# Products with the identity in transposing mode, and the second attention's probabilities normalised in place

## What is computed

```python
# _L0_cond2_ref: the conditioned layer, H = 16 heads of DH = 128
x1 = _ln(x) * (1.0 + scale1) + shift1
qkv = (x1 @ qkv_w + qkv_b).reshape(Bc, Tc, 3, H, DH)
q, k, v = (qkv[:, :, 0], qkv[:, :, 1], qkv[:, :, 2])
scale = DH ** (-0.5)
attn = jnp.einsum('bthd,bshd->bhts', q, k) * scale
attn = jax.nn.softmax(attn, axis=-1)
attn_out = jnp.einsum('bhts,bshd->bthd', attn, v).reshape(Bc, Tc, INNER)
...
x = x + _L0_attn_ref(_L0_cond_ref(cond_2048, cond_2048, x, L0_cond_coupling, L0_cond_bias), L0_attn_Wqkv_w, L0_attn_Wqkv_b)
x = x + _L0_ffn_ref(_L0_cond2_ref(x, cond_2048, ...), ...)
```

## Time and profile before

| | us |
|---|---|
| median of three runs (lowest, highest) | 6142.88 (6142.48, 6146.08) |
| the profiled execution | 6141.46 |
| its span, first to last instruction | 6139.8 |

### The profile page before, as it was taken

One profiled execution on the slowest core, in us unless ns is written; L12 is line 12 of the kernel. 1 busy time (PEld: TensorE's weight loads), 2 busy tenths in 40 slices (PEclk: granted clock), 3 DMA queues, 4 the chain that ended last, 5 costly groups with the idle time before them and its releaser, 6 DMA issues. The chain is left out here.

```text
span 6139.8 us, 221854 instructions
## 1 busy us (share of the span) xinstructions
PE 4707.2 (77%) x82040; PEld 4113.7 (67%) x82040; DVE 4180.4 (68%) x26093; ACT 2342.0 (38%) x10351; POOL 1733.9 (28%) x5906
## 2 busy tenths in 40 slices
PE   6777777777777777777689962999999999269888
PEld 5666666666666666666578861778777877158777
DVE  8999999999999999999756634544454444521122
ACT  3333333333333333333355522544444444222232
POOL 2333333333333333333332202222222122200000
PEclk6555555555555555555599965999999999579999
DMA  1000000000000000000200024222232232230211
GB/s 63 1 1 1 1 1 1 1 1 1 1 1 1 1 1 1 1 1 1 70 8 22 33 77 137 90 97 93 96 103 96 89 102 82 103 124 27 93 37 41
DMA packets 121590, 260.62 MB, mean 42 GB/s; under 512 B 10276, under 2 KB 10532, under 8 KB 121112
## 3 DMA queue, kind: packets, MB, share of 16 engines
q1 hardware_dynamic: 85072, 173.09, 8.2%
q0 software_dynamic: 13104, 48.26, 2.3%
q10 hardware_dynamic: 23064, 35.84, 1.8%
HBM read 194.20 MB, written 62.97 MB: 42 GB/s over the span
## 5 line engine op out<-in xcount | busy, mean ns | idle before, releaser
L211 PE MATMUL bank<-tanh_parts,w_lo 128*128 128x4 f16 x32768 | 1205.2, 169 | 850.5 <-ACT tanh_parts L168 849.2
L211 PEld LDWEIGHTS bank<-tanh_parts,w_lo 128*128 128x128 f16 x32768 | 1030.6, 105 | 1035.5 <-ACT tanh_parts L168 1033.6
L168 ACT ACTIVATE tanh_parts<-ys 128x8 f16<-128x8 f32 x4096 | 852.8, 208 | 1902.6 <-DVE ys L306 1902.2
L219 PE MATMUL bank<-tanh_parts,w_hi 128*128 128x8 f16 x32768 | 1206.3, 173 | 0.0
L219 PEld LDWEIGHTS bank<-tanh_parts,w_hi 128*128 128x128 f16 x32768 | 1062.4, 104 | 0.0
L169 ACT ACTIVATE tanh_full<-ys 128x8 f32<-128x8 f32 x4096 | 804.4, 196 | 0.0
L306 DVE TENSOR_TENSOR_SCAN ys<-mix,bank 128x24 f32<-128x24 f32 x4096 | 719.2, 198 | 57.1 <-PE bank L219 3.5
L298 DVE TENSOR_TENSOR tanh_parts<-tanh_full,tanh_parts 128x8 f16<-128x8 f32 x4096 | 686.8, 178 | 0.4 <-ACT tanh_full L169 0.4
L1518 POOL TENSOR_TENSOR t_w<-t_raw,t_w 128x2048 fp32r<-128x2048 f32 x64 | 292.7, 4574 | 650.6 <-ACT t_w L1538 650.6
L618 PE MATMUL t_bank<-t_x,t_w 128*128 128x512 f32 x1584 | 381.3, 393 | 55.0 <-POOL t_w L1512 55.0
L618 PEld LDWEIGHTS t_bank<-t_x,t_w 128*128 128x128 f32 x1584 | 296.7, 189 | 117.0 <-issue 55.7
(11 more groups left out here) (282 smaller groups left out, 9617.6 us busy)
## 6 DMA issues: line engine op xcount, KB each, us to landing
t_raw<-L_cond_qkv_w_dram SPq DMA_DIRECT2D x51, 1024.0 KB, 5.0
t_x<-n ACTq DMA_DIRECT2D x34, 1024.0 KB, 7.6
t_carried<-x_t POOLq DMA_DIRECT2D x17, 1024.0 KB, 5.8
t_raw<-L_cond_out_w_dram SPq DMA_DIRECT2D x16, 1024.0 KB, 5.1
x_t<-t_carried POOLq DMA_DIRECT2D x16, 1024.0 KB, 4.4
n<-n_out SPq DMA_DIRECT2D x8, 1024.0 KB, 5.6
n<-o_out SPq DMA_DIRECT2D x8, 1024.0 KB, 5.6
g_raw<-L_cond_ffn_w_dram SPq DMA_DIRECT2D x8, 1024.0 KB, 10.6
```

The costliest lines, as they stand in the source:

```text
L168: act.activation(tanh_parts[:, u, at, :, 0], ys[:, s, at, :, 2], ACT.Tanh, scale=1.0 / SCALE).then_inc(s_th, 1)
L211: pe.matmul(sums[:, :, 2], w_lo[:, w_of, k, m * P:(m + 1) * P], tanh_parts[:, u, k, :, 0], start=(m % 2 == 0 and k == 0), stop=False, skip ...
L219: last = pe.matmul(sums[:, :, 1:3], w_hi[:, w_of, k, m * P:(m + 1) * P], tanh_parts[:, u, k], start=False, stop=(m % 2 == 1 and k == C - 1 ...
```

## The change

The products with the identity get `is_transpose=True`, in all the places named above but the one for `cond_rows` (L195). Operands, banks, counts and semaphores stay. In the second attention the diagonals go: `dve_scale` multiplies each of the head's four 128x512 tiles of probabilities by its reciprocal in place, signals after each, and no longer waits for the turns of the head before; `pe_turn` turns them against the plain identity and waits for the tile's signal.

```diff
-    def pe_turn(self, pe, unit, i, parity):
-        if i == 0:
-            pe.wait_ge(self.scaled, unit + 1)
+    def pe_turn(self, pe, unit, i, parity, identity):
+        pe.wait_ge(self.scaled, unit * TT + (i + 1))
         pe.wait_ge(self.low, unit * TT + (TT + i + 1 - self.t_age[i]))
         out = self.t_bank[self.t_of[i]]
         for j in range(TT):
-            last = pe.matmul(out[:, j * P:(j + 1) * P], self.probs[:, parity, i, j * P:(j + 1) * P], self.diag[:, i, :],
+            last = pe.matmul(out[:, j * P:(j + 1) * P], self.probs[:, parity, i, j * P:(j + 1) * P], identity, is_transpose=True,
                              start=(j == 0), stop=(j == TT - 1), skip_group_check=True)
...
-    def dve_scale(self, v, unit, identity):
+    def dve_scale(self, v, unit, parity):
         v.wait_ge(self.exped, unit * TT + (TT + 2))
         v.reciprocal(self.inverse[:, :], self.sums[:, :]).then_inc(self.own, 1)
-        v.wait_ge(self.turned, unit * TT + TT)
         per_unit = 1 if self.scale == 1.0 else TT + 1
         v.wait_ge(self.own, unit * per_unit + per_unit)
         for i in range(TT):
-            last = v.tensor_scalar(self.diag[:, i, :], identity, self.inverse[:, i:i + 1], None, ALU.mult)
-        last.then_inc(self.scaled, 1)
+            v.tensor_scalar(self.probs[:, parity, i, :], self.probs[:, parity, i, :], self.inverse[:, i:i + 1], None,
+                            ALU.mult).then_inc(self.scaled, 1)
...
                 for x in range(len(ROUND_BLOCKS[k % 3])):
-                    last = pe.matmul(turn_bank[use % 2][:, x * P:(x + 1) * P], probs[:, k % 2, j, x * P:(x + 1) * P], identity[:, :],
+                    last = pe.matmul(turn_bank[use % 2][:, x * P:(x + 1) * P], probs[:, k % 2, j, x * P:(x + 1) * P], identity[:, :], is_transpose=True,
```

More of the change, by code:

```diff
@@ L181, in _ @@
                     last = pe.matmul(banks[k][:, m * P:(m + 1) * P], coup[:, m, k * P:(k + 1) * P], identity[:, :],
-                                     start=(m == 0), stop=(m == C - 1), skip_group_check=True)
+                                     is_transpose=True, start=(m == 0), stop=(m == C - 1), skip_group_check=True)
                 last.then_inc(s_tr, 1)
@@ L190, in _ @@
                     last = pe.matmul(banks[j % 4][:, c * P:(c + 1) * P], rows[:, j % 4, c * P:(c + 1) * P], identity[:, :],
-                                     start=(c == 0), stop=(c == C - 1), skip_group_check=True)
+                                     is_transpose=True, start=(c == 0), stop=(c == C - 1), skip_group_check=True)
                 last.then_inc(s_tr, 1)
@@ L487, in __init__ @@
         self.pt = [sb(name + f"_pt_{part}", [P, TT, TT, P], F32R) for part in ("hi", "lo")]
-        self.diag = sb(name + "_diag", [P, TT, P], F32)
         self.peak = sb(name + "_peak", [P, TT], F32)
@@ L923, in turn_back @@
                     last = pe.matmul(turn_bank[use % 2][:, i * P:(i + 1) * P], tokens[:, i, c * P:(c + 1) * P], identity[:, :],
-                                     start=(i == 0), stop=(i == TT - 1), skip_group_check=True)
+                                     is_transpose=True, start=(i == 0), stop=(i == TT - 1), skip_group_check=True)
                 last.then_inc(s_turned, 1)
@@ L1125, in causal_phase, with dve_pipeline @@
     nc.all_engine_barrier()
-def dve_pipeline(core, v, first, heads, low, take, identity, fill=lambda slot: None):
+def dve_pipeline(core, v, first, heads, low, take, fill=lambda slot: None):
     for u in range(heads + 2):
@@ L1143, in dve_pipeline @@
         if u < heads:
-            core.dve_scale(v, first + u, identity[:, :])
+            core.dve_scale(v, first + u, u % 2)
         fill((u, "end"))
@@ L1638, in values @@
                     core.pe_values(pe, it * GROUP + h, lambda a, j: val[a][:, j, h * DH1:(h + 1) * DH1])
-                pipeline(GROUP, scores, lambda h, i: core.pe_turn(pe, it * GROUP + h, i, h % 2), values, fill)
+                pipeline(GROUP, scores, lambda h, i: core.pe_turn(pe, it * GROUP + h, i, h % 2, identity[:, :]), values, fill)
                 pe.wait_ge(core.taken, it * GROUP + (GROUP + 1))
@@ L1688, in take @@
                                            in1=att[0][:, h, :].bitcast(F32), op0=ALU.add, op1=ALU.subtract).then_inc(core.taken, 1)
-                dve_pipeline(core, v, it * GROUP, GROUP, lambda h, i: core.dve_low(v, it * GROUP + h, i), take, identity, fill)
+                dve_pipeline(core, v, it * GROUP, GROUP, lambda h, i: core.dve_low(v, it * GROUP + h, i), take, fill)
                 v.wait_ge(s_car, 16 * it + 16)
@@ L1816, in _ @@
                             last = pe.matmul(tb[q % 2][:, c * P:(c + 1) * P], raw[:, n % RAW, c, r * P:(r + 1) * P], identity[:, :],
-                                             start=(c == 0), stop=(c == 3), skip_group_check=True)
+                                             is_transpose=True, start=(c == 0), stop=(c == 3), skip_group_check=True)
                         last.then_inc(s_tr, 1)
```

## The result

| | median us (lowest, highest) | runs |
|---|---|---|
| before | 6146.65 (6142.48, 6152.46) | 8 |
| changed | 6162.66 (6152.74, 6163.97) | 8 |

The ratio is 1.0024, with a 95% interval of 1.0015 to 1.0034: 16 us slower. The forecast was 6160. The profiled execution of the changed kernel took 6152.74 us, the lowest of its eight. In it the recurrence, in whose steps nothing was changed, lasted 2966 us from its first to its last tanh, and 2971 in the profile of before; in the ten profiles of the experiments it is anything from 2965 to 2974.

A forecast was written before the change was run, and what follows sets the result against it. PE was taken to bound both attentions and the sign layer's weight stage. Terms -43 - 19.5 - 48 + 76 + 38 + 14 = +17.5 gave 6159 for the profiled execution, 6160 for the median; range 6106 to 6190.

The forecast's parts named there:

- The lock: Second attention, step 2: fourth scaling waits out GpSimd's `t_w`, scores 4.8 us late; +76 us including width, 4 in 5.
- wider scaling: Second attention: four 512-column scalings last 1.67 us, 0.8 more; after step 2, 0.4 us a group is lost.
- the clock: Second attention: PE drops to 1.2 GHz behind idle time; +38 us behind 4.6 us waits, +14 behind tile 3's waits.
- turns of the second attention: Only tile 3's turn shortens, 0.7 us in steps 1 to 3; 0.9 saved in step 4; -48 us.
- Price of a block: Every turned 128x128 block: 0.06 us in transposing mode instead of 0.22; 0.11, the middle bound, kept in the range.
- Causal rounds: Causal attention: turn 3 starts earlier, rounds save 1.0, 1.0 and 0.7 us; -43 us, or -36 at 0.11 a block.
- Sign weights: Sign layer's weight stage: PE drops below ACT's pace, 31.8 us become 21 to 22; -10 us.
- Rival (a): Step 2's fourth scaling gets in before GpSimd, whose request counts only 0.15 us after its start; 6059, chance 0.15.
- Rival (b): Second attention: in-place scalings run at the slow pace, 0.6 us apart, beside GpSimd without waiting; 6072, chance 0.06.
- Tile 3 waits: Second attention, steps 1 and 2: PE's wait for tile 3 grows from 1.15 to about 3 us.
- (c): Second attention: turns in transposing mode do not count as work for the clock, 24 more falls, +42 us; 6202, chance 0.11.
- (d): The mode saves nothing on PE, blocks stay at 0.22 us, only the scaling's loss is left; 6257, chance 0.05.

## Why the prediction came out right, step by step

The forecast of 6160 was 2.7 us from the median. The lock, the largest term, was right in mechanism and size. But that the sum is so near is luck, because its errors cancel: the gains of the cheaper blocks were put 28 us too high (16 in the causal stage, 12 in the second attention) and the wider scaling 7 too low, the clock 35 too high.

| term | forecast | measured | from |
|---|---|---|---|
| causal stage with its weights | -47 | -31 | stage |
| small stages | -15.5 | -14 | -2.4 and -11.4, stages |
| turns of the second attention | -48 | -36 | 16 x (0.51 + 0.49 + 0.50 + 0.76) |
| wider scaling, no lock | +6 | +13 | 16 x (0.30 + 0.50) |
| lock | +70 | +70 | 16 x (15.68 - 11.29) |
| clock | +52 | +17 | 16 x (21.22 - 20.17) |

The forecast had lock and width as one term of 76, 0.4 us a group of it the width; the interval 2 to 3 grew by 4.69, 75 us in all. The lower end of the stated range, 6106, is 2 us below what its own terms give. In the third term 0.50 in step 2 to 3 is taken from its neighbours, since there it is mixed with the scaling: the interval grew by 0.30 without the lock. So the split of -36 and +13 is partly argued; their sum, -1.45 us a group, is measured (85.09 against 86.54, in groups without lock and fall).

- **Price of a block: wrong, 0.06.** The spacing is that of the middle bound. Twelve blocks in step 4 take 1.47 us, the last 0.27 of it:

```profile
4137.08 1.47 PE L538 MATMUL f_turned<-t_ident,f_probs 128*128 128x128 f32 x12
4139.40 0.66 PE L538 MATMUL f_turned<-t_ident,f_probs 128*128 128x128 f32 x4 [0.85 <-DVE f_pt_lo L584]
```

  (1.47 - 0.27) / 11 = 0.109 us. A record costs what it cost before; there is one for each block in place of two. The rows with 16-bit operands were the wrong neighbour. The Trainium skill's factor of four ("TensorE: Matmul & The Clock Gate", Terms) shows in no row here: the block got two times faster. With 0.11 the forecast's own alternative for the turns, -37, is met by -36, and that for the causal rounds, -36, nearly (48 rounds were 28.8 us per three and are 26.8: -32).
- **Causal rounds: the mechanism held, its size did not.** In a round like that of the earlier trace rows the turn of tile 3 starts 4.37 us after the round's first score instead of 4.75 (forecast 4.28), and the projection 5.24 instead of 6.02 after it (forecast 5.0). The weights gave 1.5 instead of 4: behind them PE waits for the low part of `tr`, which comes from a transfer.

```profile
3283.82 0.40 PE L874 MATMUL m_scores<-mask_h,identity_h 128*128 128x128 f16 x4
...
3288.19 0.52 PE L891 MATMUL m_turned<-ident,probs 128*128 128x128 f32 x3
...
3289.06 0.48 PE L615 MATMUL m_proj<-tr_hi,wT_hi 128*128 128x512 f32 x1
```

- **Sign weights: about right.** PE ran below ACT's pace as forecast; 23.4 us instead of 31.8, where 21 to 22 were forecast. The first eight tiles ran for the most part at the lower clock (0.58 above).
- **The lock: right in every number.** It was the fourth scaling, in all 16 groups, with 4.76 us, behind `t_w` starting 1.04 after the first, scores 4.8 late, PE idle for 4.6. Rival (a) needed a request that counts 0.15 us after its start; one that stood 0.05 ahead of the fourth scaling was counted, so (a) falls. Its outcome was near all the same: GpSimd starting 0.32 us later gives 6082 (the rival: 6059). Rival (b) falls by the pace: unhindered scalings stand 0.40 us apart (four in 1.68). Nor would the slow pace alone have helped, since the slow form with a second SBUF input is locked out too.
- **Tile 3 waits: right.** It started 4 us behind the scores, after 2.4 to 2.5 us of idle time (forecast 3; the cheaper block price had shortened the turns ahead too much). The step's text gave the period as 90, while its own terms add up to 91.6 (86.5 - 3.0 + 4.8 + 3.3); it is 90.54.
- **The clock: its falls came as forecast, their price did not.** At all 16 waits of 4.6 us (3.9 where the clock had been low ahead of them) the clock fell, and the scores behind them ran at 1.2 GHz. But I took the full loss of the earlier trace rows, where nothing waits behind the matmuls, for a place that has a wait for tile 3 behind it: 38 us forecast, about 0 measured (the intervals 15.68 and 15.75 above). The falls behind tile 3's waits were 14 of 32, not a quarter, and cost 17 us where 14 were forecast: behind the wait of step 1 no cover stands and a fall costs some 1.6 us,

```profile
4003.63 0.65 PE L538 MATMUL f_turned<-t_ident,f_probs 128*128 128x128 f32 x4 [2.37 <-DVE f_pt_lo L584]
4004.04 4.58 PE L1600 MATMUL t_bank<-t_w,t_x 128*128 128x512 f32 x12
```

  behind that of step 2 some 0.45, as the periods of 85.57 and 85.10 show with GpSimd waiting for the third scaling.
- **Rivals (c) and (d)** are out: turns count as work, and the mode halves what PE pays.

Why the clock falls behind one wait of 2.4 to 2.7 us and not behind the next one of the same length stays open; I did no run on it.

## What to carry to other kernels

Where an edit widens an elementwise instruction on DVE that has its data in SBUF, look up what GpSimd starts in the time that is added: here 0.8 us more of DVE's work cost 4.4 us a group, and a wait of 0.3 us on GpSimd's side, for an instruction that nobody was waiting for, took it back. Before a lower clock is priced, follow the chain to the next wait: a slow stretch in front of a wait can be free, as in all 16 groups here, and work put in to keep the clock up can move the fall to where it is not. And when a product gets cheaper but waits at the same semaphore, move it in the order: the mode gave 23 us in the second attention where it stood, and 82 more came from the place of one turn and the falls that went with it.

## What the runs showed of the hardware

- A float32 block in transposing mode is one record of the same pace as each of the two that a plain product has: 0.109 us at 2.4 GHz, 0.213 at 1.2 GHz (twelve in 2.76 us, the last 0.42 of it).
- A running DVE instruction does not keep the port for the next one of its queue. GpSimd's request 0.03 to 0.15 us ahead of the next instruction was enough, and that instruction then lasted 4.72 to 4.80 us instead of 0.48. A request 0.04 or 0.17 us behind its start made GpSimd wait, for 0.2 us; the first of these came while the instruction before it was still running.
- An instruction with two SBUF inputs at 0.67 us a piece is locked out just as one with a single input at 0.40.
- Blocks in transposing mode raise and hold the granted clock like products (1.00 in 5842.00 to 5858.20; 33 falls with either as filling). I had given 1 chance in 9 against that.
